# Joining the output stores of neighbouring tiles in a one-core ViT tower layer

## The chip, the core and the metric

The kernel runs on one core of one Trainium2 chip. The metric is the device time of one execution in microseconds; of the kernel before there are three timed runs, with a median of 127.58 us (127.48 to 127.99). Beside them one execution was profiled.

## What is computed

The input is 32 images of 3 x 96 x 96 float32. Each is cut into 6 x 6 patches of 16 x 16 x 3 = 768 values, which gives 1152 patches (tokens).

```
p = patches(x)                                   # (32, 36, 768)
h = layernorm(layernorm(p) @ W + b)              # (32, 36, 192)
h = h + attention(layernorm(h))                  # 12 heads of 16, over the 32 images, cosine scores, softmax
h = h + ffn(layernorm(h))                        # two quantised linear layers, 192 -> 2 x 512 -> 192, silu gate
return h                                         # out: (32, 36, 192) float32
```

The output has 32 images, 36 patches of each, 192 values of each patch: 768 bytes per token, 864 KB in all.

## The kernel before, in words

The 1152 tokens are worked on in T = 9 tiles of 128 tokens, one token per partition. A tile is named by a pair of patch rows (t // 3, so pair 0, 1 or 2) and a column c = t % 3. Its 128 partitions are four groups of 32 images: partitions 0 to 31 and 32 to 63 are the patches of the pair's two rows at column c, partitions 64 to 127 those of the same two rows at column c + 3. So the half of a tile (64 partitions) covers two patch rows and one column, for 32 images, and tiles 3k, 3k + 1 and 3k + 2 hold neighbouring columns of the same rows. In the output array neighbouring columns of a row are neighbouring 768-byte pieces.

Everything stays in SBUF until the end: `h2_all` is [128, 9, 192], so on one partition the results of tiles t and t + 1 lie side by side. All engines run hand-ordered lists of steps with a counting semaphore for each kind of step. PE does the transposes and matmuls, DVE the layer norms, softmax parts and the last addition, ACT the copies out of PSUM and the quantising steps, GpSimd (POOL) the powers, the head scaling and the products of the feed-forward part. The last step of a tile is `out_(t)` on DVE (line 1065), which writes tile t of `h2_all` in place and counts `out_ok` up. DVE runs `out_` in the order of the tiles, 0 to 8.

The queue of the SyncE engine (SP) issues nearly all loads at the start, and after them the stores. For every tile it waits until `out_ok` has counted that tile, and issues two stores by `store` (line 248), one for each half of the partitions. Of the last tile it issues one half; the other is issued by ACT behind a wait of its own (lines 564 and 565), so that the two go out side by side. SP then waits until the semaphore `stored` has counted all 18 stores, and with that the kernel ends. A store of the kernel before moves 64 pieces of 768 bytes, 48 KB; in the output array its outer dimension has 2 steps (the two patch rows) and its middle one 32 (the images).

Of the kernel before, what the change touches and what calls it, by code (L numbers as in the profile page):

```python
# [16 lines left out]
G = IMG // PS  # L17
# [3 lines left out]
D = 192  # L21
# [5 lines left out]
T = B * NPATCH // P  # L27
TG = 5
PAIRS = G // 2
WT = G // 2  # L30
# [16 lines left out]
def vit_layer(nc, x, ln1_g, ln1_b, w_emb, b_emb, ln2_g, ln2_b, w_in_proj, b_in_proj, logit_scale,  # L47
              head_scale, w_out_proj, b_out_proj, w_ff_in, g_in, w_ff_out, g_out, out):
    ctx = ExitStack()
    with ctx:  # L50
        def sb(name, shape, dt=F32):
            return ctx.enter_context(nc.sbuf_tensor(name, shape, dt))

        def sem(name):
            return ctx.enter_context(nc.semaphore(name))
# [79 lines left out]
        h2_all = sb("h2_all", [P, T, D])  # L135
# [31 lines left out]
        ld_b1, ld_emb, ld_bemb, ld_ln2, ld_ls, ld_gin, ld_gout, ld_qkv, ld_o, ld_wi, ld_wo, stored = (  # L167
            sem(n) for n in ("ld_b1", "ld_emb", "ld_bemb", "ld_ln2", "ld_ls", "ld_gin", "ld_gout", "ld_qkv", "ld_o", "ld_wi", "ld_wo",
                             "stored"))
# [67 lines left out]
        def load_x(eng, pair, js):  # L237

            for j in js:
                h, w0 = 2 * pair + j % 2, IMG // 2 * (j // 2)  # L240
                for c in range(C):
                    eng.dma_start(xs[32 * j:32 * j + 32, pair, PS * c:PS * (c + 1), :],  # L242
                                  x[:, c, PS * h:PS * (h + 1), w0:w0 + IMG // 2]).then_inc(ld_x[pair], 16)

        def store(eng, t, half):

            first = 2 * G * (t // WT) + t % WT + WT * half
            eng.dma_start(out[:, first:first + G + 1:G, :].rearrange("b j d -> j b d"),
                          h2_all[64 * half:64 * half + 64, t, :]).then_inc(stored, 16)

        block = ctx.enter_context(nc.Block())

        @block.sync
        def _(sp):

            load_x(sp, 0, (0, 1))
            sp.dma_start(b1_sb[:, :].rearrange("p (s c) -> p s c", s=2), ln1_b.rearrange("(s p c) -> p s c", s=2, c=C)).then_inc(ld_b1, 16)
            sp.dma_start(g1_sb[:, :].rearrange("p (s c) -> p s c", s=2), ln1_g.rearrange("(s p c) -> p s c", s=2, c=C)).then_inc(ld_emb, 16)
            sp.dma_start(w_emb_sb[:, :, :].rearrange("p (s c) d -> p s (c d)", s=2),
                         w_emb.rearrange("(s p c) d -> p s (c d)", s=2, c=C)).then_inc(ld_emb, 16)  # L260
            sp.dma_start(b_emb_bc[:, :], b_emb.partition_broadcast(P)).then_inc(ld_bemb, 16)
            sp.dma_start(ls_bc[:, :], logit_scale.rearrange("h a b -> (h a b)").partition_broadcast(P)).then_inc(ld_ls, 16)
            sp.dma_start(w_qkv_raw[:, :, :], w_in_proj.rearrange("(r p) d -> p r d", p=HC)).then_inc(ld_qkv, 16)
            sp.dma_start(w_qkv[HC:HC + 1, 0, :], b_in_proj.rearrange("(a n) -> a n", a=1)).then_inc(ld_qkv, 16)
            sp.dma_start(g2_bc[:, :], ln2_g.partition_broadcast(P)).then_inc(ld_ln2, 16)
            sp.dma_start(b2_bc[:, :], ln2_b.partition_broadcast(P)).then_inc(ld_ln2, 16)
            load_x(sp, 1, (0, 1, 2, 3))
            sp.dma_start(wi_raw[:, :, :], w_ff_in.rearrange("(k p) d -> p k d", p=P)).then_inc(ld_wi, 16)
            sp.dma_start(wo_raw[:, :, :], w_ff_out.rearrange("(k p) d -> p k d", p=HC)).then_inc(ld_wo, 16)
            sp.dma_start(w_o[HC:HC + 1, 0, :], b_out_proj.rearrange("(a n) -> a n", a=1)).then_inc(ld_o, 16)  # L270
            sp.dma_start(w_o_raw[:, :, :], w_out_proj.rearrange("(r p) d -> p r d", p=HC)).then_inc(ld_o, 16)
            sp.dma_start(hs_bc[:, :], head_scale.rearrange("h a b -> (h a b)").partition_broadcast(P)).then_inc(ld_o, 16)
            load_x(sp, 2, (0, 1, 2, 3))
            sp.dma_start(gin_bc[:, :], g_in.partition_broadcast(P)).then_inc(ld_gin, 16)
            sp.dma_start(gout_bc[:, :], g_out.partition_broadcast(P)).then_inc(ld_gout, 16)

            for t in range(T):
                sp.wait_ge(out_ok, t + 1)
                store(sp, t, 0)
                if t < T - 1:  # L280
                    store(sp, t, 1)
            sp.wait_ge(stored, 16 * 2 * T)

        @block.gpsimd
        def _(pool):
# [122 lines left out]
        def _(act):  # L408
# [153 lines left out]
            yqTe_half(8, 0); yqTe_half(8, 1)  # L562

            act.wait_ge(out_ok, T)
            store(act, T - 1, 1)

        @block.tensor
        def _(pe):
# [556 lines left out]
```

## Time and profile before

| | us |
|---|---|
| median of 3 timed runs | 127.58 (127.48 to 127.99) |
| the profiled execution | 127.43 |
| its span, first to last instruction | 125.5 |
| outside the span | 1.93 |
| PE, DVE, ACT and POOL busy | 106.9, 102.5, 86.1, 70.9 |
| mean granted clock of TensorE, as a share of full speed | 0.983 |

The span is what the trace covers. The 1.93 us outside it belong to the execution's time and are in no view. The busy times are sums over the whole span; all four compute engines are busy well over half of it, and no single one fills it. Of the DMA the page gives the mean busy share of 16 DMA engines: over the first quarter of the span nearly all of them are busy, after that nearly none. For reading the rows below: a share of 0.14 of 16 engines is 2.2 engines' worth of packet time.

### The profile page before, as it was taken

The page shows a single profiled execution, that of the slowest core. Times are in us where ns is not written, and L with a number is a line of the kernel's source. Part 1 is how long each engine was busy: PE and PEld are TensorE (multiplying, and loading weights), DVE is VectorE, ACT ScalarE, POOL GpSimd, SP SyncE. Part 2 cuts the span into 40 slices and gives each one's busy share as a digit, 9 for nine tenths or more (in the row PEclk, how much of TensorE's full clock was granted, in tenths as well). Part 3 has the DMA queues.
Part 4 walks back from the last instruction along what each step waited for, and adds up shares of the span by engine and source line. Part 5 has one row for each costly group of instructions (what it writes and reads, how often), then busy time and mean ns, then how long its engine had stood idle before and what let it go on. Part 6 is the DMA issues. An engine that isn't in the chain of part 4 may idle for free.

```text
span 125.5 us, 4783 instructions
## 1 busy us (share of the span) xinstructions
PE 106.9 (85%) x1851; PEld 84.7 (67%) x1854; DVE 102.5 (82%) x384; ACT 86.1 (69%) x175; POOL 70.9 (57%) x164
## 2 busy tenths in 40 slices
PE   5998998999999998999999999899989976844500
PEld 5988898799787886976776766777567743423100
DVE  4039438999999999999999999999999999967200
ACT  0406537899998853296587995985999978996500
POOL 7002007349341096175269789998899898885000
PEclk9999999999999999999999999999999999999985
DMA  4999999969700000000000000000001010110110
GB/s 83 237 272 219 177 181 275 228 120 162 136 22 3 0 5 3 5 5 3 5 5 5 0 0 5 5 5 3 5 8 28 7 43 21 30 35 21 34 46 33
DMA packets 24095, 7.77 MB, mean 62 GB/s; under 512 B 20038, under 2 KB 23495, under 8 KB 24072
## 3 DMA queue, kind: packets, MB, share of 16 engines
q1 hardware_dynamic: 20838, 6.82, 27.0%
q10 hardware_dynamic: 3234, 0.64, 2.7%
q8 instruction: 15, 0.25, 0.9%
q14 instruction: 8, 0.07, 0.2%
HBM read 6.58 MB, written 0.88 MB: 59 GB/s over the span
## 4 chain that ended last, share of the span: by engine, by line
PE 33%; DVE 25%; POOL 18%; issue 9%; DMA 4%; ACT 3%; ACTq 2%; POOLq 0%; DVEq 0%
PE bank L662 7%; POOL yw L359 5%; DMA xs<-in_x_dram 4%; PE bank L667 3%; PE bank L684 3%; POOL r L367 3%; PE bank L685 3%; PE bank L646 3%; PE bank L713 2%; ACTq L242 2%; POOL yy L351 2%; DVE ss L913 2%; PE bank L701 2%; PE bank L584 2%; DVE mx L971 2%
## 5 line engine op out<-in xcount | busy, mean ns | idle before, releaser
L662 PE MATMUL bank<-w_emb_g,xT 128*128 128x192 f32 x72 | 13.5, 330 | 1.1 <-DVE h0s L879 1.0
L866 DVE BATCH_NORM_STATS2 bst<-xs 128x6 f32<-128x384 f32 x18 | 9.0, 540 | 6.0 <-DMA xs<-in_x_dram 6.0
L315 POOL TENSOR_TENSOR rs<-mv,mhalf 128x1 f32<-128x1 f32 x9 | 5.5, 609 | 14.6 <-DVE mv L888 14.6
L662 PEld LDWEIGHTS bank<-w_emb_g,xT 128*128 128x128 f32 x72 | 11.6, 190 | 2.2 <-issue 2.0
L461 ACT ACTIVATE xp<-xs,mv 128x768 f32<-128x768 f32 x9 | 8.4, 935 | 5.7 <-DVE mv L872 5.7
L577 PE MATMUL bank<-ident 128*128 128x128 f32 x60 | 8.8, 315 | 1.8 <-POOL ident L289 1.5
L359 POOL TENSOR_TENSOR yw<-yy,gout_bc 128x512 f32<-128x512 f32 x8 | 10.2, 1271 | 0.2
L311 POOL TENSOR_TENSOR rs<-mv,mhalf 128x1 f32<-128x1 f32 x9 | 5.2, 582 | 8.8 <-DVE mv L872 8.8
L713 PEld LDWEIGHTS bank<-vx,pT 32*32 32x32 f32 x864 | 8.2, 104 | 2.3 <-issue 2.3
L577 PEld LDWEIGHTS bank<-ident 128*128 128x128 f32 x60 | 8.3, 165 | 2.0 <-POOL ident L289 1.5
L713 PE MATMUL bank<-vx,pT 32*32 32x17 f32 x864 | 8.9, 180 | 0.2 <-issue 0.2
L319 POOL TENSOR_TENSOR rs<-mv,mhalf 128x1 f32<-128x1 f32 x9 | 5.1, 564 | 6.3 <-DVE mv L909 6.3
L701 PEld LDWEIGHTS bank<-kT,qT 32*32 32x32 f32 x432 | 6.5, 104 | 3.0 <-issue 2.6
L701 PE MATMUL bank<-kT,qT 32*32 32x64 f32 x432 | 7.9, 216 | 0.4 <-DVE qT L963 0.3
L387 POOL TENSOR_TENSOR kpad<-qk,rn 128x192 f32<-128x192 f32 x9 | 4.6, 512 | 5.5 <-DVE rn L958 5.5
L684 PE MATMUL bank<-w_qkv,xhT 97*128 97x384 f32 x18 | 7.5, 496 | 0.0
L667 PE MATMUL bank<-w_emb_g,xT 128*128 128x192 f32 x36 | 7.5, 330 | 0.0
L685 PE MATMUL bank<-w_qkv,xhT 96*128 96x384 f32 x18 | 7.3, 485 | 0.0
L532 ACT ACTIVATE yq<-yw,mround,qs 128x512 f32<-128x512 f32 x8 | 6.4, 804 | 0.7 <-DVE qs L1060 0.7
L484 ACT ACTIVATE sq<-bank 128x384 f32<-128x384 f32 x9 | 4.4, 489 | 3.5 <-PE bank L685 3.5
L517 ACT ACTIVATE th<-bank,f_h 128x512 f32<-128x512 f32 x9 | 6.2, 686 | 0.9 <-PE bank L745 0.5
L879 DVE SCALAR_TENSOR_TENSOR h0s<-bank,rs,bias_emb 128x192 f32<-128x192 f32 x9 | 3.7, 409 | 3.8 <-issue 3.5
(158 smaller groups left out, 350.7 us busy)
## 6 DMA issues: line engine op xcount, KB each, us to landing
xs<-in_x_dram SPq DMA_DIRECT2D x30, 96.0 KB, 3.2
out_dram<-h_all SPq DMA_DIRECT2D x17, 48.0 KB
wi_raw<-in_L_ffn_w_in_dram SPq DMA_DIRECT2D x1, 768.0 KB, 7.5
xs<-in_x_dram ACTq DMA_DIRECT2D x6, 96.0 KB, 3.9
w_emb_sb<-in_L_tok_W_dram SPq DMA_DIRECT2D x1, 576.0 KB, 5.1
w_qkv_raw<-attn_in_proj_weight_dram SPq DMA_DIRECT2D x1, 432.0 KB
wo_raw<-in_L_ffn_w_out_dram SPq DMA_DIRECT2D x1, 384.0 KB, 8.1
gout_bc<-in_L_ffn_g_out_dram SPq DMA_DIRECT2D x1, 256.0 KB, 4.7
```

The lines of the kernel that those rows point to most:

```text
L359: nc.gpsimd.tensor_tensor(out=yw[:, s, :], in0=yy[:, s, :], in1=gout_bc[:, :], op=ALU.mult).then_inc(yw_ok, 1)
L461: nc.scalar.activation(xp[:, t % 3, :].rearrange("p (r w) -> p r w", w=PS), x_tile(t), ACT.Identity, bias=mv1[:, t, 0:1], scale=-1.0).then ...
L517: nc.scalar.activation(th[:, t % 2, :], gate_ps[:, :], ACT.Tanh, scale=f_h[:, t, :]).then_inc(th_ok, 1)
L532: nc.scalar.activation(yq[:, t % 2, :], yw[:, t % 3, :], ACT.Identity, bias=mround[:, 1:2], scale=qs5[:, t, :]).then_inc(yq_ok, 1)
L577: nc.tensor.transpose(xT_lo[:, 0:P], ident[:, :], ident[:, :])
L662: nc.tensor.matmul(emb_bank, xT[:, t % 3, P * k:P * (k + 1)], w_emb_g[:, 3 * (k % 2) + k // 2, :], start=(k == 0), stop=False)
L667: mm = nc.tensor.matmul(emb_bank, xT[:, t % 3, P * k:P * (k + 1)], w_emb_g[:, 3 * (k % 2) + k // 2, :], start=False, stop=(k == KF - 1))
L684: nc.tensor.matmul(qk_ps, xhT[:, t % 3, 0, :], w_qkv[:, 0, 0:2 * D], start=True, stop=False)
L685: nc.tensor.matmul(qk_ps, xhT[0:HC, t % 3, 1, :], w_qkv[0:HC, 1, 0:2 * D], start=False, stop=True).then_inc(qk_mm, 1)
L701: mm = nc.tensor.matmul(bank[6][q, 2 * B * a:2 * B * (a + 1)], qT[q, s, B * a:B * (a + 1)], kT[q, s, 2 * B * a:2 * B * (a + 1)], start=Tru ...
L713: mm = nc.tensor.matmul(o_bank[q, h, :], pT[q, s, B * h:B * (h + 1)], vx[q, t, h, :], start=True, stop=True)
L866: nc.vector.bn_stats(bst1[:, t, 6 * n:6 * (n + 1)], pixels[:, 24 * n:24 * (n + 1), :]).then_inc(bst1_ok, 1)
```

## The change

`store` takes a number n of tiles, and moves the same half of n neighbouring tiles at once. Each piece is n x 768 bytes, contiguous in SBUF and in the output array; there are still 64 pieces, and the outer dimension on the output side still has 2 steps, the middle one 32. SP stores tiles 0 to 2 once `out_ok` is 3, tiles 3 to 5 at 6, tiles 6 and 7 at 8, two stores each, and half 0 of tile 8 at 9. ACT still stores half 1 of tile 8. In all 8 stores take the place of 18, and the last wait is for 16 x 8. The order of the compute engines' work is unchanged.

```diff
-        def store(eng, t, half):
+        def store(eng, t, n, half):
 
-            first = 2 * G * (t // WT) + t % WT + WT * half
-            eng.dma_start(out[:, first:first + G + 1:G, :].rearrange("b j d -> j b d"),
-                          h2_all[64 * half:64 * half + 64, t, :]).then_inc(stored, 16)
+            pair, c = t // WT, t % WT
+            rows = out.rearrange("b (r h c) d -> h r b (c d)", r=G, h=2)
+            eng.dma_start(rows[half, 2 * pair:2 * pair + 2, :, D * c:D * (c + n)],
+                          h2_all[64 * half:64 * half + 64, t:t + n, :].rearrange("p t d -> p (t d)")).then_inc(stored, 16)
...
-            for t in range(T):
-                sp.wait_ge(out_ok, t + 1)
-                store(sp, t, 0)
-                if t < T - 1:
-                    store(sp, t, 1)
-            sp.wait_ge(stored, 16 * 2 * T)
+            for t, n in ((0, 3), (3, 3), (6, 2)):
+                sp.wait_ge(out_ok, t + n)
+                store(sp, t, n, 0)
+                store(sp, t, n, 1)
+            sp.wait_ge(out_ok, T)
+            store(sp, T - 1, 1, 0)
+            sp.wait_ge(stored, 16 * 8)
...
             act.wait_ge(out_ok, T)
-            store(act, T - 1, 1)
+            store(act, T - 1, 1, 1)
```

## Rows read from the trace of the kernel before

**Rows 1.** The page's head and its engines.

```profile
span 125.5 us, 4783 instructions
PE 106.9 (85%) x1851; PEld 84.7 (67%) x1854; DVE 102.5 (82%) x384; ACT 86.1 (69%) x175; POOL 70.9 (57%) x164
```

**Rows 2.** End of the chain of waits: start us, us, engine, step.

```profile
117.85 0.35 PE bank L773 x2
118.23 0.42 DVE h_all L1065
```

**Rows 3.** Waits of SP's queue: us in total, times, longest us.

```profile
SPq L248 <- DVE h_all L1065: 78.4, 8, 60.7
SPq L50 <- DMA out_dram<-h_all: 5.9, 1, 5.9
```

**Rows 4.** Stores by line: duration ns min/median/max, first and last start us.

```profile
L248 SPq DMA_DIRECT2D out_dram<-h_all x17: 511/512/639, 92.0 to 118.7; - x17
L248 ACTq DMA_DIRECT2D out_dram<-h_all x1: 1343/1343/1343, 118.7 to 118.7; - x1
```

**Rows 5.** Timeline of DVE's last step of tiles 2 to 8: start us, us.

```profile
100.94 0.41 DVE L1065 SCALAR_TENSOR_TENSOR h_all<-bank,f,h_all 128x192 f32<-128x192 f32 x1
106.00 0.41 DVE L1065 SCALAR_TENSOR_TENSOR h_all<-bank,f,h_all 128x192 f32<-128x192 f32 x1
108.79 0.42 DVE L1065 SCALAR_TENSOR_TENSOR h_all<-bank,f,h_all 128x192 f32<-128x192 f32 x1
113.31 0.41 DVE L1065 SCALAR_TENSOR_TENSOR h_all<-bank,f,h_all 128x192 f32<-128x192 f32 x1
114.40 0.42 DVE L1065 SCALAR_TENSOR_TENSOR h_all<-bank,f,h_all 128x192 f32<-128x192 f32 x1
116.28 0.42 DVE L1065 SCALAR_TENSOR_TENSOR h_all<-bank,f,h_all 128x192 f32<-128x192 f32 x1 [0.61 <-PE bank L783]
118.23 0.42 DVE L1065 SCALAR_TENSOR_TENSOR h_all<-bank,f,h_all 128x192 f32<-128x192 f32 x1 [1.53 <-PE bank L773]
```

**Rows 6.** Timeline of SP's queue: first stores of tiles 3 and 5, both of 7.

```profile
106.43 0.51 SPq L248 DMA_DIRECT2D out_dram<-h_all  x1
113.75 0.51 SPq L248 DMA_DIRECT2D out_dram<-h_all  x1
116.72 0.51 SPq L248 DMA_DIRECT2D out_dram<-h_all  x1
117.27 0.62 SPq L248 DMA_DIRECT2D out_dram<-h_all  x1
```

**Rows 7.** Windows: stretch, us, busy by engine, PEclk, DMA share, GB/s.

```profile
106.40:107.55 1.15, 0.80 (x6) 0.45 (x6) 1.01 (x3) 1.15 (x4) 1.15 (x2) 1.00 0.00 0
107.55:113.00 5.45, 3.29 (x21) 1.89 (x20) 4.44 (x12) 4.89 (x9) 4.64 (x11) 1.00 0.13 38
113.00:113.75 0.75, 0.00 (x0) 0.00 (x0) 0.71 (x4) 0.32 (x1) 0.59 (x3) 1.00 0.00 0
113.75:114.85 1.10, 0.98 (x8) 0.71 (x8) 0.98 (x2) 0.49 (x1) 0.91 (x3) 1.00 0.06 15
114.85:119.00 4.15, 2.16 (x13) 0.91 (x12) 1.43 (x5) 2.73 (x5) 0.31 (x2) 1.00 0.14 34
119.00:124.50 5.50, 0.00 (x0) 0.00 (x0) 0.00 (x0) 0.00 (x0) 0.00 (x0) 0.70 0.14 47
124.50:124.70 0.20, 0.00 (x0) 0.00 (x0) 0.00 (x0) 0.00 (x0) 0.00 (x0) 0.50 0.05 15
124.70:125.50 0.80, 0.00 (x0) 0.00 (x0) 0.00 (x0) 0.00 (x0) 0.00 (x0) 0.50 0.00 0
```

**Rows 8.** DMA packets and queues, 119 to 124.5 us.

```profile
DMA packets 342, 0.26 MB, mean 47 GB/s; under 512 B 9, under 2 KB 342, under 8 KB 342
q1 hardware_dynamic: 279, 0.21, 11.1%
q10 hardware_dynamic: 63, 0.05, 2.6%
```

**Rows 9.** The same, 114.7 to 115.3 us: the instruction queue.

```profile
q8 instruction: 1, 0.02, 10.6%
```

**Rows 10.** DMA packets and queues, 8.1 to 8.9 us, nearly all in packets over 2 KB.

```profile
DMA packets 135, 0.30 MB, mean 380 GB/s; under 512 B 1, under 2 KB 4, under 8 KB 135
q1 hardware_dynamic: 135, 0.30, 102.6%
```

**Rows 11.** DMA issues of the whole span: KB each, median us to landing.

```profile
xs<-in_x_dram SPq DMA_DIRECT2D x30, 96.0 KB, 3.2
out_dram<-h_all SPq DMA_DIRECT2D x17, 48.0 KB
```

## The prediction

> **What bounds the kernel now.** I read the page's head first: four compute engines are busy for 57% to 85% of the span [rows 1], so no single engine's total decides, and a change at the end of the program has to be read at the end of the trace. The chain of waits ends with DVE's last addition, from 118.23 to 118.65 us [rows 2], yet the span ends at 125.5. So the last 6.9 us hold no computation at all. The waits of SP's queue say what fills them: its final wait, the one for the stores, took 5.9 us [rows 3]. The reader is to see there that this is one wait, for the DMA.
>
> The next question is whether those 5.9 us are the fixed delay of one store or a line of stores being drained. The windows answer it. From 119.0 to 124.5 us the DMA moves a steady 47 GB/s at a share of 0.14 of 16 engines, and then stops within 0.2 us; after 124.7 nothing moves [rows 7]. A fixed delay would be a gap without bytes. This is a drain at full load of few engines: the share by queues is 11.1 + 2.6 = 13.7% of 16, or 2.19 engines' worth of packet time [rows 8]. In those 5.5 us it moves 0.26 MB, which is 5.3 stores of 49,152 bytes (48 KB), though only the two stores of tile 8 were issued after 118.65. The other three and more were already waiting. So **the end is set by the rate at which the queued stores drain, on about two DMA engines, and by how many bytes come into the line late.**
>
> When does that line form? The stores of tiles 3 and 4 come free at 106.41 and 109.21 [rows 5] and are through by 113.00: the window up to 113.75 shows 0 GB/s [rows 7]. The first store of tile 5 is issued at 113.75 [rows 6]. A store's first bytes come some 1.15 us after its issue: tile 3's is issued at 106.43 [rows 6], and up to 107.55 nothing moves [rows 7]. That makes 114.9 here; the 15 GB/s of the window before it are 16 kB in 1.1 us, one packet of the instruction queue [rows 9]. From then on no window is empty until about 124.65. That last stretch carries the stores of tiles 5, 6, 7 and 8: 8 x 49,152 = 393 kB.
>
> **The change part by part.**
>
> *Fewer issues and waits.* SP issues 7 stores in place of 17, at 0.51 us each [rows 4], and waits 4 times for `out_ok` in place of 9. SP has no other work, and spent 78.4 us waiting for DVE there [rows 3], so this saves nothing. The last stores' issue isn't delayed either: the pair for tiles 6 and 7 is issued from 116.72, like tile 7's now, the second one from 117.27 for 0.62 us [rows 6], to 117.9, before tile 8 is ready at 118.65. If the cover went, an issue would cost at most 0.6 us. I count 0. ACT's issue of 1.34 us [rows 4] stays as it is.
>
> *Tiles 0 to 2.* Their joined stores can be issued at 101.35 us, when tile 2 is added up [rows 5], and hold 295 kB, 6.3 us at 47 GB/s. With the 1.15 us ahead they would be through by about 109, and the next line begins at 114.9. Hidden, cost 0; the cover is some 5 us thick.
>
> *Tiles 3 and 4.* This is the term that counts. Their four stores, 4 x 49,152 = 197 kB, go out now between 107.55 and 113.00, beside computation [rows 7]. Joined to tile 5 they can't start before 113.72, when tile 5 is added up [rows 5]. They enter the last line. At the drain's rate of 47 GB/s they add 197 / 47 = 4.18 us to it.
>
> *Bigger packets.* Pieces become 2304 bytes (tiles 3 to 5) and 1536 (tiles 6 and 7). What a bigger piece gives per engine I take from packets over 2 KB near the start: 380 GB/s over 16 x 1.026 = 16.4 engines' worth, 23.1 GB/s each [rows 10]; in the drain it is 47 / 2.19 = 21.4 GB/s [rows 8]. The gain is a factor of 1.08 at most there (loads, not stores, and all 16 engines loaded), which would make 50.8 GB/s for the pair. The ends are 47 (no gain) and 50.8; as 1536 lies halfway, and the row is of loads, I take 50. Late bytes in joined stores: (6 + 4) x 49,152 = 492 kB, 9.83 us; tile 8's 98 kB stay small, 2.09 us at 47. Together 11.92 us, against 393 / 47 = 8.37 for the line of before: +3.55 us. With the ends of the rate it is +3.4 and +4.2.
>
> *Gaps in the drain.* The line takes longer than 8.37 us: from 114.9 to 124.65 it is 9.75, so 1.4 us are lost. All of that is before 119.0, where the mean is 34 GB/s and not 47 [rows 7], while stores are still being issued. If the loss goes with the issues, it is 0.17 us for each of 8; six remain, which saves 0.35. If it goes with the groups that start together, it falls by up to 0.7; if with something else, by 0. I take 0.35.
>
> **Sum:** +3.55 - 0.35 = +3.2 us. The profiled execution's own 127.43 becomes 130.6 (its span 125.5 becomes 128.7, the 1.93 outside it stay), and by the median of the timed runs, 127.58, it is **130.8 us**, 2.5% slower. The likeliest case's own ends are +2.7 (rate 50.8, gaps -0.7) and +4.4 (rate 47, gaps unchanged, 0.2 for the spread between executions): 130.3 to 132.0.
>
> **Two rules of the Trainium skill weighed here.** Both are about what a store costs. The skill (DMA: Bandwidth & Descriptors, Rules for kernel authors) advises coalescing many small transfers, since under 64 KB one pays mostly overhead; its estimate for a transfer (Anatomy of one DMA, given for the GpSimd path) is 2.0 us plus bytes at 436 GB/s. By that rule a joined 147 kB store would take an estimated 2.3 us and be done long before tile 8, and the change would cost nothing or help. The drain at 47 GB/s [rows 8] does not agree with it. The same page (Why a DMA increments its semaphore by 16 and not by 1) says that a DMA runs on the largest number of engines up to 16 which divides the slowest dimension of both access patterns; with an outer 2 on the output side that is two engines. With that the trace agrees, 2.19 engines' worth, and since the joined store keeps an outer 2, it stays at two.
>
> **The rivals.**
>
> *A. The packet is what costs, not its bytes; the time falls.* If an engine takes a fixed time per packet whatever its size, joining pays: the last line has 6 x 64 = 384 pieces in place of 512, 8.37 us becomes 6.28, and with the gap saving of 0.2 or so the end comes 2.3 us earlier: 125.3 us. The place is the two engines of the drain; it decides for faster once a joined piece (1920 bytes on average) costs under 1.5 times a 768-byte one. For it: the same number of pieces per store. Against it: in the drain a packet takes 0.137 x 16 x 5.5 us / 342 = 35 ns [rows 8], and one over 2 KB 1.026 x 16 x 0.8 us / 135 = 97 ns [rows 10], 2.8 times as long for 3 times the bytes. Chance 0.04. Beside this case stands the Trainium skill's rule of coalescing (above).
>
> *B. The joined stores are spread over more engines.* The loads of x, 96 KB each, land in 3.2 us in the median although 30 of them stand in line [rows 11], so the queue can use far more than two engines. If the new shape did, everything but tile 8 would be through by 118.7, and the end would be tile 8's two stores alone: issued at 118.67, first bytes 1.15 us later as at tile 5, 2.1 us of drain, 122.0 or so, against 124.65. That gives 125.0 us, -2.6. Against: the old shape, which differs only in the length of its pieces, drains on 2.19 engines' worth [rows 8]. Chance 0.04.
>
> *C. No change.* The 5.9 us are a fixed latency of the last store, and the queue behind is beside the point: 127.6 us. For it: the final wait names only the last event. Against: 47 GB/s without a break until 124.5 [rows 7]. Chance 0.04.
>
> **How the numbers follow.** The drain has 0.88, A, B and C have 0.04 each. What can be told from no change in this kernel is about 0.5%, 0.64 us; the whole of the drain's range lies beyond it, so slower has 0.88, faster (A and B) 0.08, same (C) 0.04. The others lie far off at 125 and 127.6, so the range is the drain's, opened a little on the low side for a pair rate that beats the loads' row: 129.8 to 132.1.
>
> **What would show it.** Right: no store traffic between the end of tiles 0 to 2 at about 109 us and 114.9; then about 47 to 51 GB/s at a share near 0.14 up to about 127.8; DVE's last addition still at 118.2; the final wait of SP about 9 us in place of 5.9; and some 640 data packets fewer, since 10 stores of 64 pieces go. Wrong in the rate: a plateau above 51 GB/s, or gaps that stay or grow. Wrong altogether: a share well above 0.14 after 114.9 (B), the joined stores drained at 70 GB/s and more (A), or a last byte where it is now (C).

## The result and the profile after

The kernel with the joined stores takes 131.97 us (131.78 to 132.37, 4 runs) where the kernel before, beside it, took 127.78 (127.48 to 128.05, 4 runs): a ratio of 1.0358 (1.0325 to 1.0391). It is slower, as forecast, by 4.2 us between the medians and 4.6 us by the ratio (0.0358 x 127.58); the forecast was 3.2. The median lies just inside the upper end of the range, 132.1, and the ratio applied to 127.58 gives 132.15, just outside: the direction came as forecast, and the loss is 1.0 to 1.4 us larger. The profiled execution took 132.01 us with a span of 130.1. Ratios, here and below, leave out an execution that is more than 1.5% slower than the fastest of its kernel; medians do not, so the last experiment's ratio, where one of four was such, is lower than its medians give.

First the waits of SP's queue, after (us in total, times, longest us):

```profile
SPq L249 <- DVE h_all L1067: 85.1, 4, 70.4
SPq L50 <- DMA out_dram<-h_all: 9.2, 1, 9.2
```

The last wait has grown from 5.9 us [rows 3] to 9.2. What fills it is in the windows of after (columns as in rows 7):

```profile
102.90:107.10 4.20, 2.61 (x15) 1.27 (x14) 4.00 (x16) 3.73 (x8) 3.84 (x8) 1.00 0.12 30
107.10:110.00 2.90, 2.62 (x16) 1.30 (x15) 2.72 (x8) 2.67 (x5) 2.55 (x7) 1.00 0.14 54
111.00:114.11 3.11, 1.57 (x9) 0.91 (x10) 2.15 (x8) 2.36 (x6) 2.58 (x8) 0.79 0.00 0
115.20:119.40 4.20, 3.28 (x16) 1.63 (x14) 1.29 (x5) 2.56 (x5) 0.32 (x2) 0.50 0.12 31
119.40:128.30 8.90, 0.01 (x1) 0.00 (x0) 0.42 (x1) 0.00 (x0) 0.00 (x0) 0.50 0.13 50
128.40:129.40 1.00, 0.00 (x0) 0.00 (x0) 0.00 (x0) 0.00 (x0) 0.00 (x0) 0.50 0.07 23
129.40:130.10 0.70, 0.00 (x0) 0.00 (x0) 0.00 (x0) 0.00 (x0) 0.00 (x0) 0.50 0.00 0
115.25:129.40 14.15, 3.24 (x15) 1.58 (x14) 1.66 (x6) 2.56 (x5) 0.27 (x2) 0.50 0.13 42
```

The reader is to see four things. Between 111 and 114.11 us nothing is stored; in the kernel before the stores of tiles 3 and 4 were on their way there, up to 113.00 [rows 7]. The line that starts at 115.25 lasts 14.15 us; that of before, from 114.90 to 124.65, lasted 9.75. Its plateau (the stretch at a steady rate) is 50 GB/s, the value that the prediction took. But its first 4.2 us give only 31 GB/s, and in its last microsecond the share halves to 0.07 at 23 GB/s. A share of 0.07 of 16 is 1.1 engines: one engine is still working and the other has nothing left.

The computation ends later too, and TensorE's granted clock is lower at the end. The last step of tiles 5 and 8 in the timeline, and the clock's row of the page (tenths of full speed in 40 slices of the span), both of after:

```profile
113.67 0.41 DVE L1067 SCALAR_TENSOR_TENSOR h_all<-bank,f,h_all 128x192 f32<-128x192 f32 x1
119.44 0.42 DVE L1067 SCALAR_TENSOR_TENSOR h_all<-bank,f,h_all 128x192 f32<-128x192 f32 x1 [1.50 <-PE bank L775]
```

and the clock's row:

```profile
PEclk9999999999999999999999999999999999855555
```

Tile 5 is ready 0.36 us later than in [rows 5] and tile 8 1.2 us later. That needed a test of its own (the repeat of the kernel before, below).

### The profile page after: what moved, and what is told of

Same layout as the page of the kernel before. It is cut to its first block, busy times and chain, and to the rows that moved or that the text cites. A ratio compares the mean times of both kernels' runs of the same rounds, so it can differ in the third digit from the quotient of the medians.

```text
span 130.1 us, 4773 instructions
## 1 busy us (share of the span) xinstructions
PE 109.0 (84%) x1851; PEld 86.5 (67%) x1854; DVE 102.5 (79%) x384; ACT 85.8 (66%) x175; POOL 70.8 (54%) x164
## 4 chain that ended last, share of the span: by engine, by line
DVE 30%; PE 27%; POOL 17%; issue 9%; DMA 4%; ACT 2%; ACTq 2%; POOLq 0%; DVEq 0%
PE bank L664 6%; POOL yw L361 5%; DMA xs<-in_x_dram 4%; POOL r L369 3%; PE bank L669 3%; PE bank L648 2%; DVE ss L915 2%; PE bank L686 2%; PE bank L687 2%; ACTq L242 2%; POOL yy L353 2%; DVE mx L973 2%; DVE sm L977 2%; DVE kT L969 2%; DVE pT L982 2%
## 5 line engine op out<-in xcount | busy, mean ns | idle before, releaser
L317 POOL TENSOR_TENSOR rs<-mv,mhalf 128x1 f32<-128x1 f32 x9 | 5.5, 608 | 14.6 <-DVE mv L890 14.6
L579 PE MATMUL bank<-ident 128*128 128x128 f32 x60 | 9.4, 336 | 1.5 <-POOL ident L291 1.5
L579 PEld LDWEIGHTS bank<-ident 128*128 128x128 f32 x60 | 9.2, 179 | 1.5 <-POOL ident L291 1.5
L761 PE MATMUL bank<-ident,yq 128*128 128x128 f32 x32 | 5.4, 295 | 2.0 <-ACT yqT L550 1.9
```

What stands on the lines that cost most here:

```text
L579: nc.tensor.transpose(xT_lo[:, 0:P], ident[:, :], ident[:, :])
```

## The experiments

Three readings were to be told apart. **Theory 1** is the prediction's: two DMA engines drain the last line, and the time is set by how many bytes enter it late. **Rival 2**: a joined store costs something by its form, late or not (a fixed amount for each joined group in its plainest form). **Rival 3**: the lower clock makes the time. Each ratio is to runs of the kernel before beside it on the same chip. The diffs show the lines that replace those of the changed kernel; the number of stores in the last wait follows.

### The same bytes late, nothing joined

```diff
-            for t, n in ((0, 3), (3, 3), (6, 2)):
+            for t, n, ready in ((0, 1, 1), (1, 1, 2), (2, 1, 3), (3, 1, 6), (4, 1, 6), (5, 1, 6), (6, 1, 7), (7, 1, 8)):
```

> Nothing is joined: all 18 stores are as before, in 768-byte pieces, but SP waits for tile 5 ahead of the stores of tiles 3 and 4 too, so that the same 590 kB fall into the last line as with the joined stores. Theory 1 (the last line drains at about 47 GB/s on two engines, and what counts is how many bytes enter it late): 12 stores of 1.05 us and 1.3 to 1.9 us of gaps from 114.9 us on, last byte near 129, 131.5 to 132.3 us in all. Rival 2 (the longer pieces, or the joined form itself, are what costs): no pieces are longer, so the time of before, 127.6. Rival 3 (the earlier fall of TensorE's clock, 0.933 mean where it was 0.983, makes the time): the clock would be 0.98 here and the time 127.6, or 0.93 and about 1.2 us more.

Measured: 131.81 us against 127.21, ratio 1.0360 (1.0328 to 1.0392), the same as the change's. Windows of this kernel:

```profile
115.40:119.50 4.10, 3.18 (x16) 1.61 (x14) 1.27 (x5) 2.57 (x5) 0.29 (x2) 0.50 0.13 33
119.50:129.50 10.00, 0.08 (x1) 0.00 (x0) 0.42 (x1) 0.00 (x0) 0.00 (x0) 0.50 0.14 46
115.40:129.55 14.15, 3.26 (x16) 1.61 (x14) 1.68 (x6) 2.57 (x5) 0.29 (x2) 0.50 0.14 42
```

The whole loss is there with 768-byte pieces in 18 stores. Holding two tiles back is enough to cost it, without any joining. And the line is as long as with long pieces, 14.15 us: here the plateau is lower, 46 against 50 GB/s, but less is lost beside it.

### Only tiles 3 to 5 joined

```diff
+            for t, n, ready in ((0, 1, 1), (1, 1, 2), (2, 1, 3), (3, 3, 6), (6, 1, 7), (7, 1, 8)):
```

> Only tiles 3 to 5 are joined; the others are stored one by one as before. Theory 1: this is the one group that makes bytes late (197 kB of them), so nearly the whole loss is here, 131.3 to 132.0 us. Rival 2 (every joined group costs something of its own): about a third to two thirds of the loss, 129 to 130.5.

Measured: 132.99 us against 127.21, ratio 1.0465 (1.0412 to 1.0518). This one group carries the whole loss, as theory 1 has it, and 1.3 us more than the middle of what was expected. In the profile the line lasts from 116.05 to 130.65, 14.6 us at 42 GB/s, 0.45 longer than the change's; the other 0.8 us lie ahead of it (tile 5 is ready at 114.91), already at tile 0, ahead of any store. Its last 1.05 us, too, is one engine alone (23 GB/s at a share of 0.07). Why the profiled execution is late from tile 0 on stays open.

### The same stores on 16 engines, tile by tile

```diff
+            for j in range(2):
+                first = G * (2 * (t // WT) + j) + WT * half + t % WT
+                q = 64 * half + 32 * j
+                eng.dma_start(out[:, first:first + n, :].rearrange("b c d -> b (c d)"),
+                              h2_all[q:q + 32, t:t + n, :].rearrange("p t d -> p (t d)")).then_inc(stored, 16)
...
+            for t, n, ready in ((0, 1, 1), (1, 1, 2), (2, 1, 3), (3, 1, 4), (4, 1, 5), (5, 1, 6), (6, 1, 7), (7, 1, 8)):
```

> Tile by tile as before, but each half is cut into two stores of one patch row: 32 partitions and 24 KB each, outer dimension 32 on both sides, 36 stores in all. Theory 1 with the two engines following from the outer dimension of 2: the stores now run on 16 engines, the line is gone, and SP's issues at 0.55 us become the limit: tile 5 from 113.72, then 14 issues, the last at about 121.4; 1.15 to the first byte, 0.5 for the completion: end of span near 123.2, time 125.2 us. If the outer dimension has nothing to do with it and the drain stays at 47 GB/s, the line is as before and the time 127.6 or more.

Measured: 125.23 us against 127.21, ratio 0.9849 (0.9829 to 0.9869); the span of 123.3 is what was expected. The window of its last line:

```profile
115.05:122.55 7.50, 2.45 (x16) 1.06 (x14) 1.69 (x6) 2.72 (x5) 0.53 (x2) 0.74 0.23 57
```

and the stores of SP's queue by line (as rows 4):

```profile
L250 SPq DMA_DIRECT2D out_dram<-h_all x34: 314/422/1305, 92.4 to 121.3; - x34
```

With 57 GB/s it is above what the pair of engines ever gave, and the last issue goes out at 121.3 us: SP's issuing is now what the end waits for.

### The same on 16 engines, joined as in the change

The row stores of the last experiment with the change's own groups.

> The joined groups of the change (0 to 2, 3 to 5, 6 and 7, and 8), each half cut into two stores of one patch row with 32 partitions, 16 stores in all. Theory 1: on 16 engines late bytes cost nothing (442 kB at over 200 GB/s are gone before tile 8), and SP has only 10 issues after 113.72, so the end is tile 8's own: last issue near 120.2 to 120.9, span 122.5, time 124.5 us, faster than the kernel before and slightly faster than the row stores tile by tile. Rival 2 (joining itself costs, the longer pieces or the late start): slower than the row stores tile by tile by 1 us or more.

Measured: 124.11 us against 127.21, ratio 0.9758 (0.9723 to 0.9793), the fastest version. Its windows:

```profile
102.20:104.15 1.95, 0.89 (x7) 0.41 (x5) 1.88 (x9) 1.49 (x3) 1.95 (x3) 1.00 0.60 151
119.00:120.75 1.75, 0.00 (x0) 0.00 (x0) 0.06 (x1) 0.00 (x0) 0.00 (x0) 0.50 0.44 113
120.75:121.60 0.85, 0.00 (x0) 0.00 (x0) 0.00 (x0) 0.00 (x0) 0.00 (x0) 0.50 0.00 0
```

SP's final wait in the same execution:

```profile
SPq L50 <- DMA out_dram<-h_all: 1.3, 1, 1.3
```

The 295 kB of tiles 0 to 2 took some 8 us on two engines (102.95 to 110.95 after) and take 1.95 us at a share of 0.60 here. The same joining that lost 3.6% on two engines is 0.9% ahead of the row stores tile by tile. This refutes rival 2 in its plainest form, a cost that a joined group has anywhere.

### Joined, but without tiles 3 to 5

```diff
+            for t, n, ready in ((0, 3, 3), (3, 1, 4), (4, 1, 5), (5, 1, 6), (6, 2, 8)):
```

> Joined are tiles 0 to 2 and tiles 6 and 7, not 3 to 5: no bytes come later into the last line than before. Theory 1: the last line holds the old 393 kB, its work is 8.15 us (piece durations 33 and 61 ns on two engines) and its gaps 1.3 to 1.9, against 9.8 in all before: the time of before within 0.3 us, 127.0 to 127.6 beside a kernel before at 127.2. Rival 2 (joining in itself costs, through its gaps or its later issue): 128.5 or more.

Measured: 129.36 us against 127.56, ratio 1.0132 (1.0088 to 1.0177). Theory 1's number fails, by more than a microsecond, and rival 2's holds. The profile shows bytes flowing from 103.20 to 126.00 with one empty stretch of 0.35 us, and after it a new line that starts slowly:

```profile
103.20:126.00 22.80, 9.60 (x58) 5.09 (x58) 12.11 (x35) 12.99 (x24) 11.00 (x25) 0.90 0.13 40
118.05:118.40 0.35, 0.20 (x3) 0.01 (x1) 0.00 (x0) 0.29 (x1) 0.00 (x0) 1.00 0.00 0
118.40:126.00 7.60, 0.34 (x2) 0.11 (x2) 0.42 (x1) 0.00 (x0) 0.00 (x0) 0.71 0.13 39
```

Tiles 0 to 2, joined, are on the two engines until 111 (as in after), and the stores of tiles 3 and 4 queue behind them. That backlog does not reach the end: it runs dry at 118.05, because tile 6 waits for tile 7. What the end waits for is the line from 118.40, 295 kB of tiles 6, 7 and 8 in 7.60 us at 39 GB/s. The kernels with only tiles 0 to 2 and only tiles 6 and 7 joined, below, tell the two groups apart.

### Joined in twos

```diff
+            for t, n, ready in ((0, 2, 2), (2, 1, 3), (3, 1, 4), (4, 2, 6), (6, 2, 8)):
```

> Joined in twos: 0 and 1, 4 and 5, 6 and 7; tiles 2, 3 and 8 alone. Half of the late bytes of the change, 98 kB of tile 4. Theory 1: the last line's work is 9.96 us, its gaps 1.4 to 2.4, so it is 1.6 to 2.6 us longer than before and the time 128.9 to 129.9: half of the change's loss. Rival 2 (a joined group costs for its piece length, late or not): the same as the kernel with 0 to 2 and 6, 7 joined, within 0.5 us.

Measured: 129.28 us against 127.56, ratio 1.0140 (1.0108 to 1.0171): +1.7 us, inside theory 1's bounds, but also equal to the last kernel, as rival 2 said. The line: 492 kB from 115.20 to 126.60, 11.4 us at 44 GB/s. It does not run dry, so it does not share the last kernel's cause; taken alone, this run does not tell the two readings apart.

### Only tiles 0 to 2 joined

```diff
+            for t, n, ready in ((0, 3, 3), (3, 1, 4), (4, 1, 5), (5, 1, 6), (6, 1, 7), (7, 1, 8)):
```

> Only tiles 0 to 2 are joined. Theory 1: their 295 kB start at 103 us in place of 93 to 100 and take 7.9 us, so that tiles 3 and 4 queue behind them and the line that the end waits for begins at 103; 18.3 us of work and 3 to 4 of gaps from 103.1 on: last byte 124.5 to 125.6, time 127.5 to 128.5. The prediction's own view (cover of 5 us, hidden) would have 127.5 too only where tiles 3 and 4 were not stored meanwhile. Rival 2 (a fixed cost per joined group): about a third of the change's loss, 129.

Measured: 127.33 us against 127.07 (10 and 13 runs), ratio 1.0013 (0.9983 to 1.0042): the same. This refutes a fixed cost for each joined group: one of three with 2304-byte pieces costs nothing where the line behind it covers it. Its line is 21.7 us for 885 kB.

```profile
103.00:124.70 21.70, 10.69 (x58) 6.09 (x58) 12.11 (x35) 12.82 (x24) 10.96 (x25) 0.74 0.13 42
```

The backlog of tiles 0 to 2 only fills the pauses that the line had before (113.00 to 114.90, [rows 7]).

### Only tiles 6 and 7 joined

```diff
+            for t, n, ready in ((0, 1, 1), (1, 1, 2), (2, 1, 3), (3, 1, 4), (4, 1, 5), (5, 1, 6), (6, 2, 8)):
```

> Only tiles 6 and 7 are joined. Theory 1: tile 6's bytes start at 117.9 us and not 116, just as tile 5's are through (114.9 + 2.8 = 117.7), so the line stands still for 0.2 us and then has 6.0 us of work and 1 to 1.4 of gaps: last byte 125 to 125.5, time 127.7 to 128.3. Rival 2 (fixed cost per joined group): 129.

Measured: 129.24 us against 127.07, ratio 1.0177 (1.0138 to 1.0216): slower than I expected by 1 us, and where rival 2 had it. Windows:

```profile
115.05:117.65 2.60, 1.82 (x11) 1.25 (x10) 1.15 (x5) 1.67 (x3) 0.29 (x2) 0.50 0.14 41
117.65:118.90 1.25, 1.11 (x7) 0.36 (x5) 0.11 (x1) 0.90 (x2) 0.00 (x0) 0.50 0.00 0
118.90:126.55 7.65, 0.32 (x2) 0.00 (x0) 0.42 (x1) 0.00 (x0) 0.00 (x0) 0.50 0.13 39
```

The engines stand idle for 1.25 us, because tile 6 waits for tile 7 (ready at 117.76 in this execution, and not at 116.70 as in rows 5, the clock being lower), and the restarted line gives 39 GB/s, with 7.65 us for 295 kB: the same line as the one from 118.40 in the kernel with tiles 0 to 2 and 6 and 7 joined (7.60 us). At 50 GB/s for the joined stores and 47 for tile 8 it would be 6.0 us. So this group accounts for the loss of both kernels, in two parts: tile 6's bytes are late, and a line that had been running stops and starts again, which loses about 1.6 us. The prediction counted neither.

### Tile 5 first

```diff
+            for t, n, ready in ((0, 3, 3), (5, 1, 6), (3, 2, 6), (6, 2, 8)):
```

> The change, with one group cut: at the moment when tiles 3 to 5 are ready, tile 5 goes first in its own two stores of 768-byte pieces, then tiles 3 and 4 joined. The last line gets the same 590 kB at the same time. In the traces so far a line that begins with a pair of stores loses 0.4 to 0.7 us where its pieces are 768 bytes, about 1.4 at 1536 and 2.2 at 2304. Theory 1b (the gaps sit in the first pair of a line and grow with the length of its pieces): the line is 11.8 us of work and 0.7 to 1.4 of gaps, 1 to 1.6 us shorter than with the change: 130.2 to 131.0 beside a kernel before at 127.5. Rival (the gaps go with long pieces wherever they stand in the line): the change's time, 131.7 to 132.0.

Measured: 131.43 us against 127.07, ratio 1.0358 (1.0313 to 1.0404), by the ratio no better than the change; the time lies between the two expectations. In the profile the line is 13.7 us (115.15 to 128.85, 44 GB/s) in place of 14.15, where theory 1b had 12.5 to 13.2. Its first 4 us and its last microsecond:

```profile
115.15:119.15 4.00, 2.13 (x13) 0.90 (x12) 1.43 (x5) 2.73 (x5) 0.28 (x2) 0.93 0.14 35
127.85:128.85 1.00, 0.00 (x0) 0.00 (x0) 0.00 (x0) 0.00 (x0) 0.00 (x0) 0.50 0.11 38
```

The end is better than after the change (38 GB/s and not 23), the start little (35 and not 31). The idea that the losses sit in the first pair and grow with the length of its pieces fails.

### Only tile 8 stored

This kernel leaves out the stores of tiles 0 to 7.

> Leaves out the stores of tiles 0 to 7; the two of tile 8 are as before, on two engines. It gives what a last store costs with no line ahead of it. Theory 1: first byte 1.15 us after 118.65, 2.1 us of work and 0.7 of gaps, 0.85 to the end of the span: span 123.4, time 125.3, 2.3 below the kernel before. If the final wait were a fixed latency (the prediction's rival C), the time of before.

Measured: 126.22 us against 127.56, ratio 0.9896 (0.9851 to 0.9941). The two stores alone:

```profile
121.10:123.85 2.75, 0.00 (x0) 0.00 (x0) 0.00 (x0) 0.00 (x0) 0.00 (x0) 0.50 0.13 36
```

and SP's final wait:

```profile
SPq L50 <- DMA out_dram<-h_all: 3.7, 1, 3.7
```

The drain is as expected; the time is 0.9 above, because tile 8 was ready at 119.84 and not at 118.65. A last wait of 3.7 us, not 5.9 or 9.2, refutes the fixed latency (the prediction's case C). And even two stores of 48 KB alone, on two engines, end later than all 16 row stores on 16: the spans are 124.6 and 121.6 us, of which 0.8 is that tile 8 was ready later here (119.84 and 119.06).

### The kernel before, once more

> The kernel before, unchanged, to see its granted clock and its spread in four more executions. Rival 3 (the change makes TensorE's clock fall earlier, 0.933 to 0.955 in its four executions): 0.98 here in all of them. Otherwise some of these are below 0.96 too, and the time does not follow the clock, since the last line starts ahead of where the fall delays the last tiles.

Measured: 127.68 us against 127.56 (10 and 13 runs), ratio 1.0008 (0.9983 to 1.0033). The mean clock of its ten executions was 0.950 to 0.970; of the thirteen of the kernel before beside it one had 0.983, and took 127.72. In its profile:

```profile
PEclk9999999999999999999999999999999999995555
```

and its windows:

```profile
114.16:115.30 1.14, 1.00 (x6) 1.00 (x7) 0.75 (x2) 0.52 (x1) 0.95 (x3) 0.50 0.05 14
115.30:124.50 9.20, 3.25 (x16) 1.60 (x14) 1.68 (x6) 2.57 (x5) 0.30 (x2) 0.50 0.14 44
```

SP's final wait:

```profile
SPq L50 <- DMA out_dram<-h_all: 4.4, 1, 4.4
```

Rival 3 falls: the kernel before takes the same time at the lower clock. The execution that the prediction rests on, at 0.983, was the uncommon one. Here tile 5 is ready at 114.16 and tile 8 at 119.93, 1.3 us later than in rows 5, and the span is 125.2, not longer: the line is not empty at any time from 115.30 to 124.50, and it covers the slower end of the computation.

### By threes on 16 engines

```diff
+            for t, n, ready in ((0, 3, 3), (3, 3, 6)):
...
+            store(sp, 6, 3, 0)
...
+            store(act, 6, 3, 1)
```

> On 16 engines (stores of one patch row, 32 partitions), joined by threes throughout: 0 to 2, 3 to 5, 6 to 8, 12 stores, the last four split between SP and ACT. All 295 kB of the last group wait for tile 8. Theory 1: on 16 engines at 130 to 170 GB/s they take 1.7 to 2.3 us after 1.15 us from the issue at 119.1: last byte 121.9 to 122.6, time 124.7 to 125.4, slightly above the version with 6 and 7 apart (124.1) but still below the kernel before, although three times as many bytes are late at the end.

Measured: 124.97 us against 127.07, ratio 0.9801 (0.9727 to 0.9875). 295 kB after tile 8:

```profile
120.60:121.85 1.25, 0.00 (x0) 0.00 (x0) 0.00 (x0) 0.00 (x0) 0.00 (x0) 0.50 0.82 236
```

At 236 GB/s three times the bytes at the very end are through in 1.25 us, where two engines need 2.75 for a third of them. Lateness is cheap where the drain is wide.

## What the prediction had right, and the step that failed

The direction and the mechanism were right, and the size was not: +3.2 us forecast, +4.2 to +4.6 measured.

**The bound: right.** The end is a line of stores draining on two engines. Three kernels with the same 590 kB in it, the one with nothing joined, the change and the one with tile 5 first, differ in pieces and in the number of stores and have lines of 14.15, 14.15 and 13.7 us and ratios of 1.036, 1.036 and 1.036. A fourth, with only tiles 3 to 5 joined, has 14.6 us and 1.0465; 0.8 us of its time lie ahead of the line. The stores cut to 32 partitions, on 16 engines, remove it. DVE's last addition was to stay at 118.2 us and came at 119.4; the line covers that, which the prediction had not considered.

**Fewer issues and waits: 0, right,** as far as the runs show: the kernel with 18 stores and the one with 8 take the same where the bytes are late alike. On 16 engines the number of issues does count (36 against 16, 125.23 against 124.11 us), and there SP's last issue, at 121.3 us, comes only 2 us before the end of the span.

**Tiles 0 to 2, hidden: right in the time, wrong in the thickness.** They were to be through by about 109 and ran to 110.95, 8.0 us at 38 GB/s and not 6.3 at 47. Alone they cost nothing (1.0013). In the change their backlog meets no stores of tiles 3 and 4; where it does, it fills up the pause.

**Tiles 3 and 4, 197 kB late: right,** and it is the term that carries the loss.

**Bigger packets: the plateau right, its worth not.** 50 GB/s was taken, 50 came; 492 kB at 50 and 98 kB at 47 are 11.9 us.

**Gaps in the drain: this is the step that failed.** The prediction tied the 1.4 us lost in the line to the issues, and had them fall by 0.35 us with their number. They rose. After: 14.15 - 11.9 = 2.25 us lost; before: 9.75 - 8.37 = 1.4, and 9.2 - 8.37 = 0.8 in the second profile. So the term is +0.9 to +1.4 and not -0.35. With the work of +3.55 that makes +4.4 to +4.9 for the line; the spans differ by 4.6 (130.1 to 125.5) and 4.9 (to 125.2). The prediction's own sign of being wrong in the rate, gaps that stay or grow, is what came.

What the runs show in its place: the loss does not go with the number of issues. With 12 stores in 768-byte pieces it is 14.15 - 590 / 47 = 1.6 us, with the change's 6 stores 2.25. It has two places. One is the start of a line on idle engines: the first 4.1 us or so give 34 GB/s before, 33 with nothing joined and 31 after, where the plateaus are 47, 46 and 50, which is an estimated 1.1, 1.2 and 1.6 us lost. The packets in the traces show it as single slow ones: in the last line of after 8 packets of 2304 bytes took 174 to 668 ns where most took 93, and with nothing joined 20 packets of 768 bytes took 66 to 333 ns where most took 36; the last of them start 3.4 and 3.5 us into the line. The other place is the end: the last microsecond after gives 23 GB/s, with one engine alone, an estimated 0.5 us lost.

So long pieces gain 0.65 us on the plateau and lose the same beside it. The change's gain from bigger packets and its gain from fewer gaps, together 1.0 us in the prediction, are both gone: 197 kB come late and cost what they cost with nothing joined. The two lines of before are 4.4 and 4.95 us shorter, 45 and 40 GB/s for those bytes, near the whole line's mean of 42 and below the plateau of 47. The mean of before's line, 393 kB in 9.75 us or 40 GB/s, was in the trace.

Whether the length of a piece sets the loss at the start is not shown. The first 4 us of four lines: tiles 0 to 2 joined in after, the same in the kernel with 6 and 7 joined too, tiles 3 to 5 joined alone (these three begin with 2304-byte pieces), and the kernel before once more (768 bytes):

```profile
102.95:106.95 4.00, 2.43 (x14) 1.15 (x12) 3.80 (x15) 3.58 (x8) 3.64 (x8) 1.00 0.12 29
103.20:107.20 4.00, 2.38 (x13) 1.19 (x14) 3.80 (x14) 3.65 (x8) 3.64 (x8) 1.00 0.12 37
116.05:120.05 4.00, 2.52 (x16) 1.14 (x14) 1.65 (x6) 2.61 (x5) 0.29 (x2) 0.93 0.14 40
115.30:119.30 4.00, 3.08 (x16) 1.60 (x14) 1.26 (x5) 2.57 (x5) 0.30 (x2) 0.50 0.14 41
```

The same group of stores starts at 29 and at 37 GB/s in two kernels, and the same kernel before at 34 and at 41 in two executions. That spread is as wide as any difference between the pieces.

**The rivals.** A (the packet costs) is refuted by the line with 384 pieces being as long as that with 768. B (spread over more engines) is not what the change does, share 0.13, but it is what the row stores do. C (fixed latency) is refuted by the last waits of 1.3, 3.7, 5.9 and 9.2 us.

**A piece missing: tile 6 waits for tile 7.** The prediction let their bytes into the line for free. In the change they find a backlog, and that is so. Where the line runs dry while tile 6 waits, the group costs 1.8% (alone) or 1.3% (with tiles 0 to 2 joined).

The Trainium skill's rule on coalescing (DMA: Bandwidth & Descriptors, Rules for kernel authors) would have joined these stores. The measurements go against it at two engines and with it at 16, 0.9% between the two row versions.

What stays open: why some packets are slow in the first microseconds of a line, why the loss differs between executions of one kernel (1.4 and 0.8 us), and why one engine is left alone at the end with the change. No run isolates these.

## What to carry to other kernels

Before joining stores, look at whether the final wait for DMA is a gap or a plateau: at a plateau the end is bytes over rate, and here the bytes that were held back until the last line cost at 40 to 45 GB/s, near the line's mean rate with its gaps and not its plateau's. Look also at whether a join lets a running line go dry: the restart cost about 1.6 us here. Look at the share of DMA engines in that plateau (0.14 of 16 here): widening the access pattern's outer dimension to 32 was worth 1.5 to 2.4%, and only then did joining pay. A computation that ends later need not matter, when such a line covers it.

## What the runs showed that I had not expected

In the profile of the repeated kernel before, TensorE's clock falls to its lower level (0.50 of full speed, 1.2 of 2.4 GHz) just before 113 us; in the profile that the prediction rests on it falls only after 121, when the computation is over. The mean clock was 0.949 to 0.984 over the 43 executions measured beside the experiments; four had 0.982 or more, and took 126.94 to 127.72 us, within the range of the rest. What TensorE did ahead of the fall at 113, in the windows of the repeated kernel (PE and PEld are the first two columns after the length, PEclk the third from the right):

```profile
110.00:111.00 1.00, 0.00 (x0) 0.00 (x0) 0.97 (x3) 1.00 (x3) 0.91 (x2) 1.00 0.10 28
111.00:112.00 1.00, 0.17 (x2) 0.20 (x3) 1.00 (x3) 1.00 (x3) 0.83 (x3) 1.00 0.12 37
112.00:113.00 1.00, 1.00 (x10) 0.71 (x8) 0.27 (x1) 0.94 (x3) 0.90 (x2) 0.91 0.13 41
113.00:114.00 1.00, 0.47 (x2) 0.00 (x0) 0.76 (x4) 0.32 (x2) 0.74 (x4) 0.50 0.05 15
```

It stood nearly idle for two microseconds, in one wait of 1.9 us for ACT. The first profile has the same wait of 1.9 us (busy 0.61 of the 2 us from 110 to 112) and kept the full clock through it, so that wait alone does not decide the fall.

In the one-row stores a median issue by SP took 0.42 us, not 0.51, but one of them took 1.7 us: the row of the joined version on 16 engines says

```profile
L250 SPq DMA_DIRECT2D out_dram<-h_all x14: 315/422/1718, 101.4 to 119.5; - x14
```
